# Mode products of half of the images at a time, inside the groups of a Fourier layer, and the inverse along the height on 64x64 quarters in all middle groups

## The reference, cut to what matters

```python
M1 = 20; M2 = 20
def _spectral_conv(x, w):
    x_ft = jnp.fft.rfft2(x, norm='ortho')
    out = jnp.einsum('bixy,ioxy->boxy', x_ft[:, :, :M1, :M2], w.astype(x_ft.dtype))
    out_ft = jnp.zeros((B, w.shape[1], H, W // 2 + 1), dtype=x_ft.dtype)
    out_ft = out_ft.at[:, :, :M1, :M2].set(out)
    return jnp.fft.irfft2(out_ft, s=(H, W), norm='ortho')

x = coords @ fc0_w + fc0_b
for sw, cw, cb in ((sw0, cw0, cb0), (sw1, cw1, cb1), (sw2, cw2, cb2), (sw3, cw3, cb3)):
    x1 = _spectral_conv(x, sw)
    x2 = jnp.einsum('bchw,oc->bohw', x, cw) + cb[None, :, None, None]
    x = _gelu(x1 + x2)
x = _gelu(x @ fc1_w + fc1_b)
return (x @ fc2_w + fc2_b)[..., 0]
```

## Time and profile before

| what | us |
|---|---|
| median of 3 runs (6322.72 to 6348.17) | 6326.73 |
| the profiled execution | 6331.26 |
| its span on the core | 6329.5 |
| TensorE busy in it | 5549.8 |
| VectorE busy | 2847.6 |
| ScalarE busy | 2686.9 |
| GpSimd busy | 1104.5 |

### The profile page before, as it was taken

How to read it: one execution, slowest core, us unless ns; L and a number is a source line. 1 busy time by engine, 2 the same in 40 slices (tenths; PEclk the granted TensorE clock), 3 DMA queues, 4 the chain that set the end, 5 groups by cost and what they waited for, 6 DMA issues and landing times. The chain is left out here.

```text
span 6329.5 us, 274083 instructions
## 1 busy us (share of the span) xinstructions
PE 5549.8 (88%) x119214; PEld 4137.1 (65%) x119214; DVE 2847.6 (45%) x4430; ACT 2686.9 (42%) x5007; POOL 1104.5 (17%) x1049
## 2 busy tenths in 40 slices
PE   5999999999899899899999999999987687888888
PEld 4876678678768776777678767767774334343343
DVE  2443344344434443444344334434442666656573
ACT  2334433443353335333433443343334546455553
POOL 3220222032212222221222122203220000000000
PEclk9999999999999999999999999999998798888887
DMA  2111111111101110211111111111110000000000
GB/s 33 14 14 14 19 14 14 15 19 14 24 8 16 23 15 10 24 14 14 19 15 14 15 19 14 14 15 17 14 14 7 17 1 8 1 8 1 4 1 4
DMA packets 442993, 85.37 MB, mean 13 GB/s; under 512 B 437592, under 2 KB 437864, under 8 KB 441704
## 3 DMA queue, kind: packets, MB, share of 16 engines
q1 hardware_dynamic: 441832, 67.58, 8.5%
HBM read 63.33 MB, written 4.23 MB: 11 GB/s over the span
## 5 line engine op out<-in xcount | busy, mean ns | idle before, releaser
L217 POOL COPY x_T<-x_X 128x512 f32<-128x512 f32 x1024 | 1075.3, 1106 | 3624.8 <-ACTq L778 3453.9
L773 ACT ACTIVATE x_X<-ga 128x512 f32<-128x512 f32 x1280 | 752.0, 598 | 1108.9 <-PE ga L452 898.9
L629 DVE COPY x_X<-ev 128x512 f32<-128x512 f32 x640 | 438.3, 688 | 872.2 <-PE ev L471 833.9
L452 PEld LDWEIGHTS ga<-pw_rhs,x_X 64*64 64x64 f32 x32768 | 592.3, 135 | 280.8 <-issue 278.8
L629 DVE COPY V<-ev 104x512 f32<-104x512 f32 x608 | 411.3, 690 | 603.7 <-PE ev L418 444.9
L483 PEld LDWEIGHTS ev<-dft_consts,x_T 128*64 128x64 f32 x16384 | 577.6, 137 | 44.1 <-issue 44.0
L483 PE MATMUL ev<-dft_consts,x_T 128*64 128x80 f32 x16384 | 597.8, 233 | 7.1 <-POOL x_T L217 5.5
L452 PE MATMUL ga<-pw_rhs,x_X 64*64 64x64 f32 x32768 | 585.2, 218 | 3.3 <-issue 2.7
L444 PE MATMUL ga<-V,inv_w 40*64 40x512 f32 x4096 | 548.6, 603 | 29.2 <-ACT V L741 27.9
L629 DVE COPY Y<-ev 128x400 f32<-128x400 f32 (+1 forms) x768 | 463.1, 603 | 209.4 <-PE ev L483 166.2
L629 DVE COPY D<-ev 128x512 f32<-128x512 f32 x576 | 362.1, 684 | 337.9 <-PE ev L390 335.6
(11 more groups left out here) (200 smaller groups left out, 8372.1 us busy)
## 6 DMA issues: line engine op xcount, KB each, us to landing
mix_w<-in_sw SPq DMA_DIRECT2D x128, 400.0 KB, 7.9
coords<-in_coords SPq DMA_DIRECT2D x64, 96.0 KB, 2.1
maps<-Y SPq DMA_DIRECT2D x128, 16.0 KB
raw<-maps SPq DMA_DIRECT2D x8, 256.0 KB, 3.4
out<-out_t SPq DMA_DIRECT2D x8, 256.0 KB, 3.1
w<-in_w SPq DMA_DIRECT2D x3, 512.0 KB, 6.9
fc_rhs<-in_fc_w SPq DMA_DIRECT2D x32, 0.4 KB
dft_consts<-in_dft SPq DMA_DIRECT2D x1, 336.0 KB
```

Source lines behind the costliest of these rows:

```text
L217: pool.tensor_copy(x_T[:, :, H * bc + h0:H * bc + h0 + 16].rearrange("p c (s n) -> p c s n", n=2), blocks.rearrange("p (s a n c) -> p a c ...
L452: last = pe.matmul(ps[HALF * bp:HALF * bp + HALF, HALF * s:HALF * s + HALF], x_X[r:r + HALF, g, col:col + HALF], pw_rhs[r:r + HALF, :], st ...
L629: dve.tensor_copy(dst, src).then_inc(ev_taken, 1)
L773: x_new = act.activation(blocks.rearrange("p (s a n) -> p s a n", s=8, a=2)[:, :, bc, :], ga[n % N_GA][:, :].rearrange("p (s n) -> p s n", ...
```

## The change

`MIX_N` becomes 16: a mode product takes the 8 images of one half (groups 0 and 1, or 2 and 3). The set for the first half stands in group 2 of the phase that makes the spectra, the set for the second half in group 0 of the next phase. `mode_fifth` has the fifth slot alone, two banks `ga`, and `mode_pair` the other four slots, two calls with one `ev` and one `ga` bank each. They stand between the steps of the group. `turn_d` of the next group is now inside every group, that of group 3 too (for group 0 of the next layer), and the inverse along the height of group 0 is four `inverse_h_pair` in the loop; in "first" two of its four parts stay 104x104 (`inverse_h_rows`) and two are on quarters. `next_layer` runs group 0's `inverse_w_and_pointwise` before the jump back. The first half of the projection of the next chunk's first group goes to the end of "last" (`run("lead")` does it once ahead of the loop). SyncE's loads of `mix_w` wait for the second half's products. Banks are counted on from one phase to the next by an offset (`EV_OFF`, `GA_OFF`).

```diff
--- before.py
+++ after.py
-MIX_N = 2 * CHUNK
+HC = CHUNK // 2
+MIX_N = 2 * HC
...
+                ends = kind == "mid" or kind == "last"
+                off = [EV_OFF, GA_OFF, -N_EV] if ends else [0, 0, 0]
...
+                def modes_begin(to, s_at):
                     pe.wait_ge(mixw_in, (chunk * LAYERS + to + 1) * (16 * J))
-                    def fifth(ps, k0, k, signal=None):
+                    pe.wait_ge(ev_taken, ev0 + s_at + 1)
+                    passed()
...
+                def mode_fifth(h, part):
+                    ps = ga_tile()
+                    passed()
+                    for k in range(MIX_K):
+                        at = MIX_K * part + k
                         for jj in range(2):
...
+                            row = slice(HALF * jj, HALF * jj + HALF)
+                            last = pe.matmul(ps[row, MIX_N * k:MIX_N * k + MIX_N], mix_w[row, (KG - 1) * M + at, :],
+                                             S[row, 0, KG - 1, HC * h:HC * h + HC, 2 * at:2 * at + 2],
+                                             start=True, stop=True)
+                    last.then_inc(ga_ready, 1)
...
+                def mode_pair(h, p, to):
+                    pair = [ev_tile()]
+                    passed()
+                    pair.append(ga_tile())
+                    passed()
+                    for k in range(M):
+                        for jj, ps in enumerate(pair):
+                            row = slice(HALF * jj, HALF * jj + HALF)
+                            for cc in range(2):
+                                kg = 2 * p + (jj ^ cc)
+                                last = pe.matmul(ps[HALF * cc:HALF * cc + HALF, MIX_N * k:MIX_N * k + MIX_N],
+                                                 mix_w[row, kg * M + k, :],
+                                                 S[row, 0, kg, HC * h:HC * h + HC, 2 * k:2 * k + 2],
+                                                 start=True, stop=True)
+                            if k == M - 1:
+                                last.then_inc(ga_ready if jj else ev_ready, 1)
+                        if p == 0 and k == 0:
+                            pe.matmul(pair[0][:, 0:MIX_N], ident[0:CH, :], dc_bias[:, bass.ds(to, 1), 0:MIX_N]
+                                      .rearrange("p a b -> p (a b)"), start=False, stop=True, skip_group_check=True)
+                def modes_taken(g):
+                    pe.wait_ge(ev_taken, ev0 + mode_ev(kind, 1, g) + 2)
+                    pe.wait_ge(ga_taken, ga0 + mode_ga(kind, 1, g) + 2)
...
-                        shared = g == 0 and i % 2
-                        ps = ga_tile() if shared else ev_tile()
+                        ps = ev_tile()
...
+                def inverse_h_rows(d_at, i):
                     pe.wait_ge(ev_taken, ev0 + d_at[0] + 1)
                     pe.wait_ge(ga_taken, ga0 + d_at[1] + 1)
-                    for i in range(INV_T):
-                        ps = ga_tile() if shared and i % 2 else ev_tile()
+                    for bank in range(2):
+                        ps = ga_tile() if bank else ev_tile()
+                        passed()
                         for s in range(4):
...
+                            last = pe.matmul(ps[0:HALF + KR, P * s:P * s + P],
+                                             D[0:HALF + KR, 8 * i + 4 * bank + s, 0:HALF + KR],
                                              inv_h[0:HALF + KR, :], start=True, stop=True)
+                        last.then_inc(ga_ready if bank else ev_ready, 1)
...
                     fc1(0)
                     if more:
                         inverse_h_pair(d_at, 0, shared=False)
+                    if g == 0:
+                        modes_begin(layer, 0)
+                        mode_fifth(1, 0)
+                        mode_fifth(1, 1)
                     x_at.append(turn_x(g, range(TURN_X // 2, TURN_X), written))
                     if more:
                         inverse_h_pair(d_at, 1, shared=False)
+                    if g == 0:
+                        mode_pair(1, 0, layer)
                     fc1(1)
                     if more:
                         inverse_h_pair(d_at, 2, shared=False)
+                    if g == 0:
+                        mode_pair(1, 1, layer)
...
-                v_at = None
-                if kind != "first":
-                    pe.wait_ge(ev_taken, ev0 + MIX_V + 1)
-                    pe.wait_ge(ga_taken, ga0 + MIX_S + 1)
+                def middle(g, d_at, half, to):
+                    written = n["ga"] - NB
+                    for i in range(INV_T // 2):
+                        turn_x(g, range(2 * i, 2 * i + 2), written)
+                        if i < INV_T // 2 - 1:
+                            inverse_h_pair(d_at, i)
+                        if half is not None and i == 0:
+                            modes_begin(to, MID_EV[g])
+                            mode_fifth(half, 0)
+                            mode_fifth(half, 1)
+                        if half is not None and i == 1:
+                            mode_pair(half, 0, to)
+                    y_at = forward_w(g)
+                    v_at = inverse_h_pair(d_at, INV_T // 2 - 1)
+                    if half is not None:
+                        mode_pair(half, 1, to)
+                    forward_h(y_at)
+                    return v_at
+                def next_layer(v_at):
+                    nonlocal ev0, ga0
+                    pe.wait_ge(ev_taken, ev0 + v_at[0] + 1)
+                    pe.wait_ge(ga_taken, ga0 + v_at[1] + 1)
                     passed()
-                    v_at = inverse_h(turn_d(0))
-                if kind == "first":
-                    project_coords(0, range(NB // 2))
...
+                if kind == "mid":
+                    v_at = middle(0, (TURN_D, 2), 1, layer)
+                    for g in range(1, NG):
+                        def behind():
+                            if g % 2:
+                                modes_taken(g - 1)
+                            return turn_d((g + 1) % NG)
+                        d_at = inverse_w_and_pointwise(g, v_at, behind)
+                        v_at = middle(g, d_at, None if g % 2 else 0, layer + 1)
+                    next_layer(v_at)
+                    return
+                project_coords(0, range(NB // 4, NB // 2))
+                for g in range(NG - 1):
                     turn_x(g)
+                    if g == 2:
+                        modes_begin(0, 2 * (TURN_V + FWD_W + FWD_H))
+                        mode_fifth(0, 0)
+                        mode_fifth(0, 1)
+                    project_coords(g + 1, range(NB // 4))
                     y_at = forward_w(g)
+                    if g == 2:
+                        mode_pair(0, 0, 0)
+                    project_coords(g + 1, range(NB // 4, NB // 2))
+                    if g == 2:
+                        mode_pair(0, 1, 0)
                     forward_h(y_at)
+                written = n["ga"] - NB
+                turn_x(NG - 1, range(TURN_X // 2), written)
+                modes_taken(2)
+                d_at = turn_d(0)
+                turn_x(NG - 1, range(TURN_X // 2, TURN_X), written)
+                y_at = forward_w(NG - 1)
+                for i in range(INV_T // 2):
+                    v_at = (inverse_h_rows if i < 2 else inverse_h_pair)(d_at, i)
+                forward_h(y_at)
+                next_layer(v_at)
+            run("lead", 0, 0, 0, None)
...
-                def mix():
...
+                def mode_pair(p, g, half):
+                    z = ev_tile()[:, 0:M * MIX_N].rearrange("p (k b r) -> p b k r", k=M, r=2)
+                    dve.wait_ge(ga_ready, ga0 + mode_ga(kind, p, g) + 1)
+                    s = S[:, :, 2 * p, HC * half:HC * half + HC, 0:KR].rearrange("p s b (k r) -> p s b k r", r=2)
+                    dve.tensor_scalar(s[:, 1, :, :, 1], z[:, :, :, 0], -1.0, None, ALU.mult)
+                    dve.tensor_copy(s[:, 1, :, :, 0], z[:, :, :, 1])
+                    take(s[:, 0], z)
...
-                if kind != "first":
-                    mix()
-                    turn_d(2)
-                    inverse_h()
...
+                if kind == "mid":
+                    for g in range(NG):
+                        half = None if g % 2 else 1 - g // 2
                         turn_d()
                         for i in range(INV_T // 2):
                             turn_x(g, [2 * i])
+                            if g == NG - 1 and i == 0:
+                                weights(layer + 1)
                             if i < INV_T // 2 - 1:
                                 inverse_h_pair(i)
+                            if half is not None and i == 1:
+                                mode_pair(0, g, half)
                         forward_w()
                         inverse_h_pair(INV_T // 2 - 1)
+                        if half is not None:
+                            mode_pair(1, g, half)
                         forward_h(g)
```

(36 more changed lines are left out.)

319 lines of the change are left out of this document (149 added, 170 removed).

## The result

| | before | changed |
|---|---|---|
| median, us | 6327.94 (4 runs) | 6840.54 (4 runs) |
| profiled execution, us | 6331.26 | 6847.76 |
| its span, us | 6329.5 | 6846.0 |
| mean granted TensorE clock | 0.937 | 0.878 |

The changed kernel is slower by a factor of 1.0803 (95% interval 1.0782 to 1.0824): 513 us, where 107 were forecast, and the range ended at 6560. Every median here is over fast runs: one run of 10719.84 us of the kernel before and one of 20045.78 us of the changed kernel with long runs read are left out.

The account below looks back on a forecast made before the run. TensorE's own stream bounds the kernel; layer ends, doubled records and jump give -20.2 us a chunk, instruction pauses +27, clock +7: +13.8 a chunk, +110 in all, some 6435 us. Own range 6360 to 6530, 8 in 10: 6250 to 6560.

Parts of the forecast that it names:

- 4.6 + 2.9 + 2.3 + 4.3: Layer end after the change: forward_w, forward_h, one turn_d and the inverse along the height on quarters, summed to 14.2 us.
- packets of 3.75 to 4.1 us: Time per packet of TensorE instructions assumed for the forecast's own range, 6360 to 6530 us.
- What bounds it: Whole kernel: TensorE's own stream, busy 88% of the span, no other engine for half; only layer ends are soft.
- Part 1: Layer ends: 14.2 us left of each, 15.5 in "first", 58 us a chunk; waits for Y, D and V go.
- Part 2: Mode products: records double to 800 a layer, priced per record whatever the columns, 15.6 us a layer, 62.4 a chunk.
- Part 3: Loop jump, now behind group 0's channel product: 3.4 us plus 1.7 of slow clock, twice a chunk, 10 us.
- Part 4: Groups with a mode set: TensorE waits for instructions, one packet per 3.87 us, +27 us a chunk.
- Longer plain groups: Sign against the forecast: groups without a mode set get longer, which nothing in the profile led it to expect.
- Rival B: Instruction refills keep up and pauses are hidden: faster, -13 to -20 us a chunk, 6165 to 6221 us; chance 0.22.
- Part 5: Granted clock in the mode sets: five falls a chunk at 1.3 us, +7 us a chunk.
- Rival D: Clock stays low through the mode sets, +34 us a chunk, with the pauses +41 in all, 6650 us; chance 0.10.

Follow-up runs that it names:

- the runs on the supply of instructions: Changed kernel with one mode product in four at 256 columns, 6304.26 us; 64 columns read in runs of eight, 6581.03; that with 104x104 inverse beside sets, 6496.59.

## Why the prediction was right or wrong

The direction was right and the size was not: +64 us a chunk in place of +13.8. The direction isn't luck alone: with the clock kept up by 64 columns the kernel is still 3.8 to 4.3% slower, by doubled records and pauses. But at 16 columns it came mostly from the clock, and not from the pauses that I had put highest. Two slips in the sums don't touch this: 4.6 + 2.9 + 2.3 + 4.3 is 14.1, and packets of 3.75 to 4.1 us give 6375 to 6560 by the prediction's own terms, not 6360 to 6530.

- **What bounds it:** right. In the changed kernel TensorE is busy for 90% of the span and no other engine for half.
- **Part 1, what is left of a layer end:** right in its steps. The waits on D and V are gone. One of 0.85 us came back, for the copy of `forward_h`, 3.4 us a chunk, since the new count of banks waits for it; I had put nothing for waits there.
- **Part 2, the records:** right. The clean pitch is 0.583 us for 40 records of `mode_pair` and for 20 of `mode_fifth`, 14.6 and 29.2 ns as forecast, and work rose by 19.5 us a chunk, where the sum has about 20 (sets 62.4 less the 29.3 of before, the inverse 11 less, and 2.5 of changes of step that count as rest here). 64 columns cost nothing when read in long runs, 2.5 ns a record in short ones. The page "TensorE: Matmul & The Clock Gate" of the Trainium skill, section "Back-to-back issue gap", has about 25 ns for a small product. The trace doesn't agree: 14.6 ns on four quarters, 29.2 on two.
- **Part 3, the jump:** right in place and nearly in size: 16 waits of 3.5 to 4.2 us, 59.8 us in all, where I had 3.4 each (the other 8 of the 24 in the row above are short). Its slow clock was wrong: 1.7 us of loss each, where 17 to 24 of the 25 us behind a jump ran at 1.2 GHz.
- **Part 4, the pauses:** the mechanism is shown by the runs on the supply of instructions and by when the pauses end, the term was too small. At full clock a group with a set takes 39.3 us where I had 37.9, and a plain group behind it 28.6 instead of 26.4: I had treated each group alone, but pauses run over into the plain ones. Longer plain groups were what I had said would show the forecast wrong, and they came: 29.12 and 28.43 us in the changed kernel. With the 64-column runs rest stands 13.5 to 17.5 us above before, where my sum has it 13 below (13.8 less 20 of work and 7 of clock). In the changed kernel itself rest is 5 below before: the slow clock hides most of it. Rival B, and "mostly hidden" of the Trainium skill, page "Runtime: NRT & Kernel Launch", section "Instruction fetch mechanics", are refuted for such streams.
- **Part 5, the clock: the step that failed.** I counted five falls of 1.3 us, +7, and took the fall for a matter of pauses and of `mode_fifth`'s half array. It is +50.7: 125 stretches at 1.2 GHz in place of 39, some 11 more a chunk, at 4.7 us each. Two things were missed. Half the columns were priced at "worth nothing" in Part 2, which holds for the time of a record at full clock and not for the clock: the kernel before had shown the mode products at 1.00 with 32 columns, and had shown no product of 16. And a low clock doesn't end with the set that caused it: `turn_x`, the quarters and `forward_h` behind it ran at 1.2 GHz too. Rival D (6650 us, above the range's end, at 0.10) named the low clock, but its +34 was for the set's own records, and not for what stands beside them.

Clock and work, 50.7 and 19.5 us a chunk, account for the 513 us between them. How the -5 of rest divides into pauses that the slow clock covers and waits that went, the traces don't part.

## What to carry to other kernels

Halving the columns of a product whose time hangs on its record and not on its columns (14.6 ns here) buys nothing and doubles the records and instructions; count instructions per us, not only array time, before small products are moved into a stream that is full. When products get narrower, price the clock as well, for the steps beside them too, and try the same stream with idle columns filled: it is a one-line experiment that parts clock from everything else. A step that wins in one place (quarters inside a group) can lose behind a stall, where the clock is low.

## What the runs showed of the hardware that I had not expected

- With the same instructions the granted clock over a group with a set was 0.76 to 0.77 with 16 columns a product, and 0.92 to 0.96 with 64, and 1.00 in a group 2 read in long runs. Moving more data made the kernel faster by 3.5%.
- Behind the jump, 104x104 products of 128 columns ran at 1.00 and 64x64 quarters of 64 columns at 0.62.
- 800 records take 23.9 us at 2.4 GHz and 25.2 us near 1.2 GHz: at the low clock TensorE is busy for 24.7 of them, at the high one for 16, and then mostly the supply of instructions sets the time.
- Pauses that no semaphore ends are over 1.25 to 1.56 us after a packet of the instruction queue has landed, in nine of ten cases.
- Behind a jump 17 to 24 of 25 us ran at 1.2 GHz with products of 16 columns, 3.4 to 6.6 with 64.
- Reading 64 columns as runs of two numbers cost some 17 ns a record at full clock, as runs of eight 14.6.
